# Keys of two tiles in even steps, queries of the two in odd steps: regrouping the projections of a pipelined attention stage

## What is computed

```python
q, k, v = proj(wq, bq), proj(wk, bk), proj(wv, bv)      # x here is layernorm(x)
attn = softmax(einsum('bhqd,bhkd->bhqk', q, k) / sqrt(hd))
o = einsum('bhqk,bhkd->bhqd', attn, v)
align = sum(o * v, -1) / (sum(v * v, -1) + EPS)
o = o - align * v
x = x + einsum('bsd,ed->bse', o, wo) + bo
```

## Time and profile before

| | |
|---|---|
| three runs | 506.61, 508.00, 508.39 us; median 508.0 |
| the profiled execution | 506.74 us, of which the span is 504.7 us |
| busy over the span | PE 491.6 (97%), PEld 396.4, DVE 335.8, ACT 335.1, POOL 246.0 |
| stages, by PE's rows | context to about 106, attention to about 345, experts to the end |
| granted clock of PE | full (1.00) throughout the attention stage |

### The profile page before, as it was taken

The page is one execution under the profiler, slowest core; times in us unless marked ns, Lnnn a source line. Parts: engine busy times, 40 slices in busy tenths (PEclk is TensorE's granted clock), DMA queues, the critical chain, the costliest instruction groups (busy, mean ns, idle before and its releaser), DMA issues.

```text
span 504.7 us, 14219 instructions
## 1 busy us (share of the span) xinstructions
PE 491.6 (97%) x4278; PEld 396.4 (79%) x4279; DVE 335.8 (67%) x1027; ACT 335.1 (66%) x814; POOL 246.0 (49%) x432
## 2 busy tenths in 40 slices
PE   8999999998999999999999999989999999999995
PEld 6545555566888888888888888768989999999995
DVE  3566665657889989898998999988553233233232
ACT  2766666569998899889888988876453433433432
POOL 2468754344344465565646556542763323333333
PEclk9999999999999999999999999999999999999999
DMA  8969997500001222322232112154657666675630
GB/s 311 272 194 291 281 314 189 172 1 2 1 3 38 85 69 75 95 95 65 77 94 79 35 59 64 56 191 149 205 197 243 199 222 210 202 224 181 199 125 19
DMA packets 35682, 70.41 MB, mean 140 GB/s; under 512 B 6753, under 2 KB 22243, under 8 KB 35633
## 3 DMA queue, kind: packets, MB, share of 16 engines
q1 hardware_dynamic: 31744, 60.72, 39.9%
q0 software_dynamic: 3456, 8.85, 4.6%
q10 hardware_dynamic: 432, 0.26, 0.2%
HBM read 58.93 MB, written 11.61 MB: 140 GB/s over the span
## 4 chain that ended last, share of the span: by engine, by line
PE 86%; DVE 4%; issue 4%; ACT 2%; POOL 2%; DMA 1%; SPq 0%; POOLq 0%; ACTq 0%; DVEq 0%
PE psum L1524 13%; PE psum L1537 12%; PE psum L1450 10%; PE psum L1429 6%; PE psum L1416 5%; PE psum L1408 5%; PE psum L1479 5%; PE psum L1276 5%; PE psum L1376 5%; PE psum L1338 3%; PE psum L1347 3%; PE psum L1295 3%; PE psum L1298 3%; PE psum L1351 3%; PE psum L1316 2%
## 5 line engine op out<-in xcount | busy, mean ns | idle before, releaser
L1524 PEld LDWEIGHTS psum<-arena,ring 128*128 128x128 f32 x640 | 77.2, 192 | 3.4 <-issue 1.4
L1524 PE MATMUL psum<-arena,ring 128*128 128x128 f32 x640 | 78.2, 275 | 0.8 <-issue 0.8
L1537 PE MATMUL psum<-w_s,arena 128*128 x320 | 75.9, 381 | 0.0
L1025 DVE TENSOR_TENSOR arena<-psum,tok 128x256 f32<-128x256 f32 x40 | 17.0, 424 | 85.4 <-PE psum L1537 84.1
L1209 ACT ACTIVATE arena<-psum 128x256 f32<-128x256 f32 x40 | 15.4, 384 | 86.9 <-PE psum L1276 59.0
L549 POOL TENSOR_TENSOR ov<-o_n,v_s 128x256 f32<-128x256 f32 x32 | 26.1, 816 | 76.2 <-DVE o_n L789 76.2
L1537 PEld LDWEIGHTS psum<-w_s,arena 128*128 128x128 f32 x320 | 57.8, 190 | 6.5
L1175 ACT ACTIVATE arena<-kT,head_mask 128x256 f32<-128x256 f32 x128 | 59.2, 530 | 0.0
L607 POOL DMA_INDIRECT out<-arena,token_of x40 | 39.9, 998 | 19.5 <-POOL token_of L599 14.3
L1215 ACT ACTIVATE arena<-psum,b_s 128x128 f32<-128x128 f32 x160 | 45.4, 374 | 3.8 <-PE psum L1524 2.2
L1139 ACT ACTIVATE arena<-arena 128x1024 f32<-128x1024 f32 x32 | 33.8, 1057 | 19.5 <-DVE arena L907 19.5
(11 more groups left out here) (206 smaller groups left out, 1095.9 us busy)
## 6 DMA issues: line engine op xcount, KB each, us to landing
ring<-w SPq DMA_DIRECT2D x40, 512.0 KB, 3.6
w_s<-ctxT SPq DMA_DIRECT2D x15, 768.0 KB, 8.3
w_s<-w SPq DMA_DIRECT2D x16, 448.0 KB, 3.3
slot_rec<-routed SPq DMA_DIRECT2D x40, 132.0 KB, 3.2
tok<-x SPq DMA_DIRECT2D x16, 256.0 KB, 8.5
w_s<-xT SPq DMA_DIRECT2D x12, 256.0 KB, 6.0
routed<-pad_rec SPq DMA_DIRECT2D x1, 1980.0 KB, 8.9
tok<-b SPq DMA_DIRECT2D x14, 128.0 KB, 3.0
```

Of the source, the lines that this page charges most:

```text
L1524: mm = pe.matmul(hid_bank(p)[:, f * P:(f + 1) * P], w1_s[:, r, c * F + f * P:c * F + (f + 1) * P], xgT[:, p, c * P:(c + 1) * P], start=c = ...
L1537: mm = pe.matmul(bank(2 + q, D), hidT[:, q, f * P:(f + 1) * P], w2_s[:, bass.ds(e * (FC * D) + f * D, D)], start=f == 0, stop=f == FC - 1)
```

## The change

Only the attention stage is touched. Tiles are taken in pairs (i, i+1) with i even.

- PE projects the keys of both tiles in the even step and the queries of both in the odd step, each as one set of four products with 256 moving columns (`project_pair`), in the place ahead of the output projection. The separate query projection between the output projection and the turning of the probabilities is gone. Each set fills bank 4, so the queries wait until the keys are copied out (`k_ok`), and the keys until the queries are (`q_ok`).
- PE turns `xn` of two tiles (i+2 and i+1 counted from the odd step, i.e. the next pair) in the odd step, as four transpositions over all of bank 5 (`turn_pair`); the even step has none. The wait for `q_ok` moves from ahead of the scores to ahead of this.
- ACT copies keys (even step) or queries (odd step) in two instructions of 256 columns, and `xnT` in one of 512 columns in odd steps. `kT` and `qT` have room for one pair; `xnT` for two pairs.
- DVE normalises a tile one step earlier, in the same place of its list.

```diff
--- before.py
+++ after.py
@@ -208,15 +208,15 @@
         open_rstd = sb("open_rstd", [P, 2, 2])
         vnorm = sb("vnorm", [P, 2, 2])
         xn = sb("xn", [P, 2, D])
-        xnT = sb("xnT", [P, 2, D])
+        xnT = sb("xnT", [P, 2, KC, 2, P])
...
-        qT = sb("qT", [P, 2, KC * P])
-        kT = sb("kT", [P, 2, KC * P])
+        qT = sb("qT", [P, KC, 2, P])
+        kT = sb("kT", [P, KC, 2, P])
...
@@ -754,7 +754,7 @@
                     ones_of_values()
 
             def attention_step(i, k, parts=("tile", "ranked", "lcs", "sums", "late"), aside=()):
-                t, u, y, w, z = i + 1, i - 1, i - 3, i - 4, i - 5
+                t, u, y, w, z = i + 2, i - 1, i - 3, i - 4, i - 5
                 if "tile" not in parts:
                     u = y = w = NT
                 r = (k - 4) % RING
@@ -778,7 +778,7 @@
                 def normalise(t, p):
                     if isinstance(t, int):
                         need(dve, s["std_ok"], t // 2 + 1 if t < RLO else NB)
-                    need(dve, s["xT_psum"], t - 1)
+                    need(dve, s["xT_psum"], t - p)
                     dve.tensor_scalar(xn[:, p, :], rows(t), mean[:, bass.ds(t, 1)], rstd[:, bass.ds(t, 1)],
                                       ALU.subtract, ALU.mult).then_inc(s["xn_ok"], 1)
                 if live(y):
@@ -789,12 +789,10 @@
                     dve.tensor_tensor(o_n[:, :].rearrange("p (h d) -> p h d", h=NH), o_ps[:, :, 0:HD],
                                       rsum[:, :].unsqueeze(2).broadcast_to([P, NH, HD]), ALU.mult)\
                         .then_inc(s["on_ok"], 1)
-                if live(t) and not (isinstance(t, int) and t in (1, 2)):
-                    normalise(t, (k + 1) % 2)
-                if isinstance(i, int) and i == 0:
-                    normalise(2, 0)
                 if isinstance(i, int) and i == -1:
-                    normalise(1, 1)
+                    normalise(0, 0)
+                if live(t):
+                    normalise(t, k % 2)
                 if "counts" in aside:
                     aside["counts"]()
                 if live(w):
@@ -1153,19 +1151,21 @@
                     .then_inc(s["vd_ok"], 1)
 
             def attention_step(i, k):
-                p, t, u, v, y, z = k % 2, i + 1, i - 1, i - 2, i - 3, i - 5
-                if live(i):
-                    need(act, s["qk_psum"], i + 1)
+                p, t, u, v, y, z = k % 2, i + 2, i - 1, i - 2, i - 3, i - 5
+                if live(i) and p == 0:
+                    need(act, s["kd_ok"], i)
+                    need(act, s["k_psum"], i + 2)
                     for c in range(KC):
-                        last = act.activation(kT[:, p, c * P:(c + 1) * P], bank(4)[:, c * P:(c + 1) * P],
-                                              ACT.Identity, bias=bk_s[:, c:c + 1])
-                    last.then_inc(s["k_ok"], 1)
-                if live(i):
+                        last = act.activation(kT[:, c, :, :], bank(4)[:, c * 2 * P:(c + 1) * 2 * P].rearrange(
+                            "p (j n) -> p j n", j=2), ACT.Identity, bias=bk_s[:, c:c + 1])
+                    last.then_inc(s["k_ok"], 2)
+                if live(i) and p == 1:
+                    need(act, s["q_psum"], i + 1)
                     need(act, s["s_psum"], i - 1)
                     for c in range(KC):
-                        last = act.activation(qT[:, p, c * P:(c + 1) * P], bank(4)[:, (KC + c) * P:(KC + c + 1) * P],
-                                              ACT.Identity, bias=bq_s[:, c:c + 1])
-                    last.then_inc(s["q_ok"], 1)
+                        last = act.activation(qT[:, c, :, :], bank(4)[:, c * 2 * P:(c + 1) * 2 * P].rearrange(
+                            "p (j n) -> p j n", j=2), ACT.Identity, bias=bq_s[:, c:c + 1])
+                    last.then_inc(s["q_ok"], 2)
                 if live(v):
                     copy_probabilities(v, p)
                 if live(z) and k % GROUP == 0:
@@ -1173,17 +1173,18 @@
                 def spread_keys(places):
                     for g in places:
                         last = act.activation(kd[:, p, :, :, g * S:(g + 1) * S],
-                                              kT[:, p, :].rearrange("p (c b j) -> p c b j", c=KC, b=2), ACT.Copy,
+                                              kT[:, :, p, :].rearrange("p c (b j) -> p c b j", b=2), ACT.Copy,
                                               scale=head_mask[:, g:g + 1])
                     return last
                 if live(i):
 
-                    need(act, s["k_ok"], i + 1)
+                    need(act, s["k_ok"], i + 2 - p)
                     spread_keys((0, 1))
-                if live(t):
-                    need(act, s["xT_psum"], t + 1)
-                    need(act, s["val_psum"], t - 1)
-                    act.activation(xnT[:, 1 - p, :], bank(5, D), ACT.Copy).then_inc(s["xT_ok"], 1)
+                if live(t) and p == 1:
+                    need(act, s["xT_psum"], i + 3)
+                    need(act, s["val_psum"], i - 1)
+                    act.activation(xnT[:, (k + 1) // 2 % 2, :, :, :].rearrange("p c j n -> p (c j n)"), bank(5), ACT.Copy)\
+                        .then_inc(s["xT_ok"], 2)
                 if live(i):
                     spread_keys((2, 3)).then_inc(s["kd_ok"], 1)
                 if live(u):
@@ -1381,6 +1382,13 @@
                 need(pe, s["of_ok"], y + 1)
                 turn(bank(5), o_f[:, q, :], s["oT_psum"])
 
+            def turn_pair():
+                for c in range(KC):
+                    for j in range(2):
+                        at = (2 * c + j) * P
+                        mm = pe.transpose(bank(5)[:, at:at + P], xn[:, j, c * P:(c + 1) * P], ident[:, :])
+                mm.then_inc(s["xT_psum"], 2)
+
             def rank_group(last):
                 rank_ps = bank(7)[:, 400:400 + GROUP * E].rearrange("p (t e) -> p t e", t=GROUP)
                 need(pe, s["ranked_ok"], last - 3)
@@ -1418,23 +1426,21 @@
                 mm.then_inc(s["wo_psum"], 1)
 
             def attention_step(i, k):
-                p, t, u, v, y, w = k % 2, i + 1, i - 1, i - 2, i - 3, i - 4
+                p, m, t, u, v, y, w = k % 2, k // 2, i + 2, i - 1, i - 2, i - 3, i - 4
 
                 def scores(c):
-                    q = (k - 1) % 2
+                    q = 1 - p
                     for b in range(2):
                         h = slice(b * S, (b + 1) * S)
                         for g in range(2):
                             r = slice(g * RG, (g + 1) * RG)
                             mm = pe.matmul(bank(g)[h, c * HG * S:(c + 1) * HG * S],
-                                           qT[r, q, c * P + b * S:c * P + (b + 1) * S], kd[r, q, c, b, :],
+                                           qT[r, c, q, b * S:(b + 1) * S], kd[r, q, c, b, :],
                                            start=True, stop=True)
                     return mm
 
                 def before_scores():
                     if live(u):
-                        q = (k - 1) % 2
-                        need(pe, s["q_ok"], u + 1)
                         need(pe, s["kd_ok"], u + 1)
                         need(pe, s["centred"], u)
 
@@ -1443,30 +1449,31 @@
                         scores(0)
                         scores(1).then_inc(s["s_psum"], 1)
 
-                def project_tile(weight, m):
+                def project_pair(weight, signal):
                     for c in range(KC):
-                        at = (m * KC + c) * P
                         for d in range(KC):
-                            mm = pe.matmul(bank(4)[:, at:at + P], weight[:, d, c * P:(c + 1) * P],
-                                           xnT[:, p, d * P:(d + 1) * P], start=d == 0, stop=d == KC - 1)
-                    return mm
+                            mm = pe.matmul(bank(4)[:, c * 2 * P:(c + 1) * 2 * P], weight[:, d, c * P:(c + 1) * P],
+                                           xnT[:, m, d, :, :].rearrange("p j n -> p (j n)"), start=d == 0, stop=d == KC - 1)
+                    mm.then_inc(signal, 2)
 
                 if isinstance(i, int) and i == NT:
+                    need(pe, s["q_ok"], i)
                     before_scores()
                     all_scores()
                     need(pe, s["l1_ok"], i)
                     project(w, p)
                     return
                 ramp = isinstance(i, int) and i < 3
-                if live(i):
-                    need(pe, s["xT_ok"], i + 1)
+                if live(i) and p == 0:
+                    need(pe, s["xT_ok"], i + 2)
                     need(pe, s["q_ok"], i)
-                    project_tile(wk_s, 0)
+                    project_pair(wk_s, s["k_psum"])
+                if live(i) and p == 1:
+                    need(pe, s["k_ok"], i + 1)
+                    project_pair(wq_s, s["q_psum"])
                 if live(w):
                     need(pe, s["l1_ok"], i)
                     project(w, p)
-                if live(i):
```

(17 more changed lines are left out.)

## The result

The changed kernel takes 512.95 us (median of four, 511.79 to 513.82) against 507.99 (four, 506.61 to 508.39) measured beside it: a ratio of 1.010, 95% interval 1.0073 to 1.0126. It is slower by 1%, where 512.8 was forecast. The profiled execution took 512.49 us with a span of 510.7, which is 6.0 more than the span before.

A forecast was written before the change was run, and what follows sets the result against it. PE looked like the bound, with a nearly closed chain through DVE and ACT. Start +1.3, steps 4 to 7 +0.4, five groups +3.4, end +0.5 sum to +5.6 us: 512.8 us, range 507.5 to 516.5.

The forecast's parts named there:

- The reckoning of needs against allowance: Attention steps: DVE/ACT chain needs 7.63, 8.04, 7.26, 7.43 us against PE's shortened step; four steps 0.69 us slower.
- the five groups: Steps 8 to 27 of the attention stage, in groups of four steps: +3.4 us together.
- A: Rival: the chain through DVE and ACT decides, taking DVE's list as rigid; 512.8 us, 510.5 to 515.5; chance 0.60.
- B: Rival: PE's own list decides, the chain has unseen air; 505.1 to 506.1 us; chance 0.16.
- C: Rival: the chain decides only at k = 1, or the end absorbs; 509 to 510.5 us; chance 0.15.
- E: Rival: weight loads bound the projections, eight wide records take eight narrow ones' 0.90 us; 481 us; chance 0.01.
- The second wait: PE's value projection waits for the router logits to leave bank 6: 0.12 us where the main stall is below 0.12.
- Width: PE's key and query projections: 1.73 us per wide group, 0.12 us saved a pair, 1.9 over 16 pairs.
- Rival D: ACT's copies or queries are late too, 0.3 us in each of 16 odd steps on top; 517.6 us; chance 0.08.
- The start: First scores wait for step 1's queries and the fourth tile's `xn`, from 114.91 to about 116.2: +1.3 us.
- Steps 4 to 7: Attention steps with little bookkeeping: stalls of 0.12, 0.26, 0.12, 0.26 us, less shorter PE work and waits: +0.4 us.
- From span to median: +5.6 us gives 512.3 on the profiled execution, 513.6 on the median; the new median was put between, 512.8.

The follow-up runs named there:

- experiment 3: The kernel of experiment 1 with every product of 256 columns replaced by two of 128; 507.01 us, ratio 1.0006 to the kernel before.
- experiment 1: The changed kernel with the pair projection cut in two halves and the output projection between them; 505.94 us, ratio 0.9984 to the kernel before.
- the form with two inputs: The changed kernel with an unread DVE addition (`tensor_tensor`) added per step: ahead of `rec` 519.89 us, ratio 1.0257; behind the statistics 518.48, ratio 1.022.
- the added reduction: The changed kernel with an unread head-wise DVE reduction added per step: ahead of `rec` 512.89 us, ratio 1.0109; behind the statistics 515.69, ratio 1.0162.
- the second form ahead: The changed kernel with an unread one-input DVE `tensor_scalar` added in every step ahead of `rec`; 517.60 us, ratio 1.0205 to the kernel before.
- experiments 2: The kernel before with only the output projection moved behind the query projection, no pairs or wide products; 513.02 us, ratio 1.013.
- experiment 5: The kernel of experiment 1 with step 1's turning of the second `xn` pair moved behind the scores of tile 0; 506.13 us, ratio 0.9981.
- experiment 6, on experiment 5: The kernel of experiment 5 with step 32's output projection of tile 28 put ahead of the last scores; 503.76 us, ratio 0.9936 to the kernel before.
- experiment 6, on before: The kernel before with step 32's output projection of tile 28 put ahead of the last scores; 505.70 us, ratio 0.9967.

## Why the prediction was right

**The reckoning of needs against allowance** (the allowance is what PE has of its own work between sending the output projection and turning the probabilities) was the step that carried it, and it held at its size. Forecast 29.73 us for four steps, measured 29.79, and the five groups +3.88 against +3.4. Step by step, forecast and measured stall ahead of the turning: k = 1 0.63 and 0.65, k = 2 0.09 and 0.14, k = 3 0.26 and 0.16, k = 0 none and none. They sum to 0.98 and 0.95. The large stall followed by a small one is that of a chain over two steps, where the stall of one step forgives the next; that k = 3 stands out over k = 2, as forecast (0.26 against 0.09), is hardly seen.

Two things in the reckoning were weaker than they read. The need's first part, from where the projection stops to `rec`, was put at 0.24; it is 0.32, 0.32, 0.20 and 0.20 in steps 16 to 19, so 0.24 was near the mean and right for none. And the check on the kernel before, "the trace confirms the reckoning there", confirms nothing: 0.32, 3.97 and 3.83 are the distances between four rows that follow each other (226.47, 226.79, 230.76, 234.59), so they add up to 8.12 whatever decides the last start. The test of the reckoning is the changed kernel and the experiments.

The doubt noted under A, that DVE's list may not be rigid, is answered for these steps: from `rec` to the maximum it took 3.56, 3.99, 3.19 and 3.47 us at k = 0 to 3, against 3.56, 3.97, 3.19 and 3.36 reckoned from before. The last part, from the maximum to the turning, is 3.81 or 3.82 in the three stalled steps, against 3.83. B and C, which have the chain decide nowhere or only at k = 1, are out by 29.79 us and by the stall at k = 3; E is out by 1.73 us a group.

**The second wait** (e, the value projection for the logits) was put at 0.12 in steps with k = 0. In step 16 the turning's slot is 0.97 (223.30 to 224.27) instead of 0.88, so 0.09; in step 20 it was 0.20.

**Width** of 1.73 per group was right (222.39 - 220.66): 0.216 us a record at 256 columns, 0.11 at 128. By the Trainium skill's "TensorE: Matmul & The Clock Gate", "Back-to-back issue gap", a wider product costs much less than in proportion. These float32 products don't show that. Experiment 3 puts the gain at 0.07 a pair, 1.1 us in all, where 0.12 and 1.9 stood in the sum; the term was too large because the group behind takes some of it back.

**Turning of `xn`**: 0.53 in odd steps as forecast, and in even ones 0.10 (0.09 was taken) for the switch to the scores, which shows in the values group (239.37 to 240.38, 1.01 instead of 0.91).

**ACT** costs nothing, as said. What it saved went into its wait: for the centring ahead of the exponential it stood 28.2 us in 32 waits, 19.5 in 31 before. Two copies of 256 columns took 0.82 to 0.84 together, within the 0.62 to 0.93 of the bounds, and PE's waits list none for the keys or queries. Rival D is out.

**The start** was the right mechanism. DVE and PE in step 1, against the earlier trace rows:

```profile
115.53 0.41 DVE L782 TENSOR_SCALAR xn<-tok,mean,rstd 128x256 f32<-128x256 f32 x1
116.00 0.66 PE L1389 MATMUL psum<-ident,xn 128*128 128x128 f32 x4 [0.97 <-DVE xn L782]
116.58 1.09 PE L1437 MATMUL psum<-arena,qT 64*64 64x256 f32 x16
```

The queries are copied at 115.44 and PE stands 0.97 for the fourth tile's `xn`. The scores come at 116.58, against 116.2 forecast and 114.91 before: +1.67, of which +0.41 was there at step 0. The remaining 1.26 are the forecast 1.3, and up to step 4 the stretch gained back 0.15 of them.

**Where sizes were off.** Steps 4 to 7 got +0.16, not +0.4. That sum was 0.76 of stalls less 0.34 of work and waits. The stalls were the larger miss. The distances from output projection to turning in steps 4 to 7 are 0.92, 1.10, 0.91 and 1.09, so the two stalls put at 0.26 are 0.19 and 0.18, and of the two waits put at 0.12 next to nothing is seen (turning's slots of 0.89). That is 0.4 in all for 0.76, while PE's own list and waits shrank by 0.2 instead of 0.34. DVE needs less there than was taken, 3.10 from `rec` to the maximum in steps 4 and 6 against 3.19. Steps 8 to 27 got 0.5 more than the sum: the five groups took 145.07 before, 0.03 a group less than the one I read, and 148.95 now, 0.06 a group more than forecast. Without the 0.41 of scatter the kernel lost 5.6 us, exactly the sum, which its parts meet less well (+1.1, +0.2, +3.9, +0.4 against +1.3, +0.4, +3.4, +0.5): errors of both signs, and that the total is exact is luck.

**From span to median** I put the forecast between the 512.3 and the 513.6 that the two bases give. The profiled executions differ by 5.75 us, the medians by 5.0, so a place between the two was right, but nothing in the prediction gave its size: the 512.8 was a choice, and that it lies 0.15 us from the measured median is luck. What makes the before-kernel's executions on that chip differ is not on record; on the chips of the experiments executions differ by the clock of the last section.

## What to carry to other kernels

A busy share near 100% on one engine doesn't say that a chain through others is far from closing. Before a group is moved on the busiest engine, write down for each value that leaves it and comes back how long the round trip needs (by the distances between starts in the other engines' lists) and how much of its own work the engine has between sending and waiting: the smaller the rest, the less that place may move. Here 0.83 us of order cost 1.2% (the changed kernel against experiment 1), while all that the wider products saved was 0.2%; cutting the wide group in two kept the width and lost none of the order.

## What was unexpected of the hardware

**DVE beside POOL.** The same DVE instruction on inputs in SBUF took 0.40 us alone and 0.82 when it started inside a POOL elementwise product (rows above), the form with two inputs 0.41 and 0.95; the added reduction took 0.40 to 0.42 in either case. Where the DVE instruction started first, in the last four steps of the second form ahead, it took 0.40 although POOL's product began beside it. The Trainium skill's "SBUF — State Buffer", "Who interferes with whom", says that DVE and GpSimd share a port pair as an exclusive lock, which elementwise operations with two inputs in SBUF and `tensor_scalar` in its fast forms can meet and a `tensor_reduce` on trn2 never does. The rows agree in which of the three are held, with 0.4 to 0.5 us as the price here; whether `tensor_scalar` ran in a fast form no row shows.

**The clock after a stand.** PE stands 1.57 us ahead of the last scores in the kernel before and in that of experiment 1 alike. In the profiled run of the second, the granted clock fell behind it. Windows view of 335 to 340 us, granted clock in the third column from the end, the kernel before first:

```profile
335.00:340.00 5.00, 3.43 (x34) 2.66 (x33) 3.49 (x10) 2.44 (x5) 1.27 (x2) 1.00 0.96 300
```

```profile
335.00:340.00 5.00, 4.18 (x27) 3.20 (x28) 2.70 (x8) 2.06 (x4) 0.73 (x1) 0.71 0.93 289
```

And PE's timeline of experiment 1 there:

```profile
335.82 1.10 PE L1437 MATMUL psum<-arena,qT 64*64 64x256 f32 x16 [1.57 <-DVE arena L905]
336.85 1.97 PE L1424 MATMUL psum<-wo_s,oT 128*128 128x270 f32 x4
338.61 0.63 PE L1277 MATMUL psum<-ident,arena 128*128 128x128 f32 x2
339.04 1.76 PE L1377 MATMUL psum<-ident,arena 128*128 128x128 f32 x8
```

The output projection's slot is 1.76 instead of the 1.01 that it has at this place in the kernel before, and the turning's 1.59 instead of 0.87: the engine ran at 1.2 of 2.4 GHz. With the two turns (0.43 for 0.22) that is some 1.7 us. Of the twelve profiled runs with this stand (1.51 to 1.57 us) six show the fall, in one of them already inside the stand, and six don't: among these last the kernel before, the changed kernel and experiments 2 and 3.

The mean granted clock of each execution tells how often. It can be parted into two groups, 0.992 to 0.996 and 0.997 to 1.000, with the medians of the times apart accordingly:

| kernel | at 0.996 or less | their median, us | above | their median, us |
|---|---|---|---|---|
| before (on the chips of the experiments) | 13 of 66 | 508.34 | 53 | 506.75 |
| experiment 1 | 6 of 12 | 506.73 | 6 | 505.39 |
| experiment 3 | 5 of 12 | 507.80 | 7 | 506.56 |
| experiment 5 | 10 of 12 | 506.23 | 2 | 505.22 |
| experiment 6, on experiment 5 | 0 of 6 | | 6 | 503.75 |
| experiment 6, on before | 0 of 12 | | 12 | 505.70 |

So the edit at the end does two things: the shorter stand (505.70 against 506.96, the 13 executions of the kernel before with the high clock on the same chip, 1.3 us), and no execution with the low clock any more, 0 of 18 where the same kernels without it had 23 of 78. That the low mean is this fall and no other is shown only for the profiled runs: the six with the fall have means of 0.993 to 0.996, the six without 0.997 to 0.999. Why the same stand is followed by a fall in some executions and not in others stays open.
